# Rotary embedding of q: cosine and sine products summed by GpSimd ahead of a smaller product with the 192 rows

## The reference

```
# D=256, K=128 per head, D_CQ=192, D_C=64, R=64
q_hk   = (hidden_q @ Wq.T)                      # per head 128
q_big  = einsum('bshk,hkq->bshq', q_hk, w_kc_q) # per head 192
q_big  = q_big*cos + rotate_half(q_big)*sin     # 192 rows, halves of 96
kv_r   = rope(kv_c)                             # 64
q_r    = einsum('bshq,hqr->bhsr', q_big, W_qr)  # per head 64
k_r    = einsum('bld,hdr->bhlr', kv_r, W_kr)
attn   = softmax(einsum('bhsr,bhlr->bhsl', q_r, k_r))
ctx    = einsum('bhsl,bld->bhsd', attn, kv_r)   # then w_kc_kv and Wo
```

## Time and profile before

| | |
|---|---|
| median of 3 runs | 559.76 us (558.8 to 560.43) |
| span of the profiled execution | 556.6 us |
| TensorE (PE) busy | 514.5 us, 92% |
| VectorE (DVE) busy | 416.5 us, 75% |
| ScalarE (ACT) busy | 307.4 us, 55% |
| GpSimd (POOL) busy | 153.4 us, 28% |
| chain that ended last | PE 64%, DVE 22% |

### The profile page before, as it was taken

The page is one execution under the profiler, slowest core; times in us unless marked ns, Lnnn a source line. Parts: engine busy times, 40 slices in busy tenths (PEclk is TensorE's granted clock), DMA queues, the critical chain, the costliest instruction groups (busy, mean ns, idle before and its releaser), DMA issues.

```text
span 556.6 us, 9071 instructions
## 1 busy us (share of the span) xinstructions
PE 514.5 (92%) x2842; PEld 391.6 (70%) x2842; DVE 416.5 (75%) x1106; ACT 307.4 (55%) x766; POOL 153.4 (28%) x152
## 2 busy tenths in 40 slices
PE   6888899998988998799999999999999988799995
PEld 3766678776867885467777777777776766588874
DVE  5988799977677668998888888888887875544322
ACT  3743654424544542577777777776777744055541
POOL 0042456755435721000000000010000007335560
PEclk9959999999999999899999999999999997999998
DMA  8668612222412329581708080807004602334426
GB/s 258 199 181 283 206 58 85 86 71 72 140 60 70 102 56 241 112 198 34 168 24 181 13 190 9 194 11 167 0 2 168 298 1 95 96 90 121 134 67 226
DMA packets 40280, 66.34 MB, mean 119 GB/s; under 512 B 4323, under 2 KB 30637, under 8 KB 39984
## 3 DMA queue, kind: packets, MB, share of 16 engines
q1 hardware_dynamic: 37984, 61.62, 39.6%
q0 software_dynamic: 2256, 4.21, 2.4%
HBM read 39.40 MB, written 28.39 MB: 122 GB/s over the span
## 4 chain that ended last, share of the span: by engine, by line
PE 64%; DVE 22%; DMA 4%; ACT 4%; issue 3%; POOL 1%; SPq 1%; POOLq 0%; DVEq 0%
PE bank L1524 10%; PE bank L792 8%; PE bank L1544 5%; PE bank L1595 5%; PE bank L1582 5%; PE bank L1571 4%; PE bank L996 4%; PE bank L827 3%; PE bank L1561 3%; PE bank L1548 2%; PE bank L1562 2%; DVE xn L355 2%; PE bank L1012 2%; DMA moe_x<-xn_slots 2%; DVE hid L748 2%
## 5 line engine op out<-in xcount | busy, mean ns | idle before, releaser
L1744 ACT ACTIVATE silu<-bank,negm 128x256 f32<-128x256 f32 x128 | 59.4, 472 | 10.3 <-DVE negm L2019 10.2
L1396 POOL TENSOR_TENSOR att_w_l<-att_w_raw,att_w_h 128x384 fp32r<-128x384 f32 x16 | 16.7, 1047 | 146.0 <-ACT att_w_h L1773 146.0
L2019 DVE TENSOR_REDUCE negm<-bank 128x2 f32<-128x512 f32 x64 | 43.9, 686 | 13.5 <-PE bank L1562 13.0
L709 POOL TENSOR_TENSOR ffn_w_l<-ffn_raw,ffn_w_h 128x512 fp32r<-128x512 f32 x30 | 39.6, 1322 | 47.5 <-ACT ffn_w_h L721 47.3
L733 ACT ACTIVATE hid_h<-hid 128x512 fp32r<-128x512 f32 x28 | 17.7, 631 | 54.9 <-DVE hid L748 49.2
L1757 ACT ACTIVATE probsT<-bank 128x512 f32<-128x512 f32 x64 | 38.0, 593 | 12.6 <-PE bank L1571 11.2
L1561 PE MATMUL bank<-ks_h,qs 128*128 128x256 f32 x128 | 40.5, 340 | 3.7 <-ACT silu L1744 2.1
L1751 ACT ACTIVATE hid<-silu,rden 128x256 f32<-128x256 f32 x55 | 27.8, 506 | 23.1 <-DVE rden L2024 23.1
L1571 PE MATMUL bank<-ident,hid 128*128 128x128 f32 x256 | 38.9, 275 | 1.2 <-DVE hid L2029 0.8
L792 PE MATMUL bank<-xT_h,ffn_w_h 128*128 128x512 f32 x120 | 39.5, 410 | 0.0
L951 POOL DMA_INDIRECT y_rows<-moe_y,route_rows x31 | 30.2, 973 | 32.8 <-issue 16.8
(11 more groups left out here) (247 smaller groups left out, 1347.6 us busy)
## 6 DMA issues: line engine op xcount, KB each, us to landing
xn_slots<-blank SPq DMA_DIRECT2D x8, 2056.0 KB, 12.8
ffn_raw<-in_w_ffn SPq DMA_DIRECT2D x30, 256.0 KB, 2.6
pair_w<-in_pair_w SPq DMA_DIRECT2D x8, 768.0 KB, 6.0
moe_w<-in_w_moe SPq DMA_DIRECT2D x1, 6144.0 KB, 18.0
folds<-att_w_raw SPq DMA_DIRECT2D x6, 704.0 KB, 7.2
moe_x<-xn_slots SPq DMA_DIRECT2D x31, 128.5 KB, 2.1
ffn_raw<-in_w_ffn SPq DMA_DIRECT2D x30, 128.0 KB, 2.3
att_w_raw<-folds SPq DMA_DIRECT2D x6, 384.0 KB, 12.1
```

Source lines behind the costliest of these rows:

```text
L709: nc.gpsimd.tensor_tensor(wt_l[b][:, 0:GU], raw[b][:, 0:GU], wt_h[b][:, 0:GU], ALU.subtract).then_inc(self.wgl, 1)
L1744: last = nc.scalar.activation(ex[u % 2][:, h, :], bank[4 + u % 2][:, h * S:(h + 1) * S], ACT.Exp, bias=negm[:, u % 2, h:h + 1], accum_out= ...
L2019: nc.vector.tensor_reduce(negm[:, u % 2, :], bank[4 + u % 2][:].rearrange("p (h n) -> p h n", h=2), AX_X, ALU.max, negate=True).then_inc(s ...
```

## The change

The sum of cosine and sine product, which TensorE made by adding up in PSUM, is made by GpSimd. For that the sine product has to lie on the partitions of its partner, so the 192 rows of each head are put in another order (`turned_order`): row r and its partner r +- 96 are 64 partitions apart in each tile. The order is applied to the weights and the tables on the host.

- `cos_sin`: every tile gets one product with cosine over 128 partitions into plane 0, and two products with sine over 64 partitions, each written to the other half's partitions of plane 1.
- `turned` (new, GpSimd): plane 0 += plane 1, 128x512, one per tile, 48 in all; in slot n for the tile of VectorE's slot n-1, ahead of `low_part`. The six of pair 0 stand before and after the splits of the next layer's weights.
- `rope_step`: two steps of two matmuls instead of three, on plane 0; they wait for `turned`.
- Folds: G has 4 blocks of 64 columns instead of 6; `fold` makes four products instead of six. `fold_out` copies the q product in two pieces per k (256 and 128 columns, rearranged) instead of one of 384. The rope weights' input shrinks from 896 to 640 columns over 64 partitions, the stored fold from 1408 to 1280 columns.

Normalising, the softmax, the values and the output are as they were.

```diff
-PR = 2 * 2 * CQ + 2 * C
+PR = 4 * P + 2 * C
-FOFF = GOFF + 2 * JT * C
+FOFF = GOFF + 4 * C
...
+                def turned(i, n):
+
+                    pool.wait_ge(s_cs, i * (4 * JT) + 2 * (n + 1))
+                    nc.gpsimd.tensor_tensor(qr[n][:, 0, :], qr[n][:, 0, :], qr[n][:, 1, :],
+                                            ALU.add).then_inc(s_turned, 1)
+
                 def slot(n, lap):
+                    tile = lap.cos_tile(n - 1)
+                    if tile is not None:
+                        turned(lap.i, tile)
                     m = lap.weights(n)
...
+                turned(0, 0)
+                turned(0, 1)
                 for st in (ffn1_first, ffn1_second):
                     ffn1.low_gateup(pool, st)
+                for n in range(2, 2 * JT):
+                    turned(0, n)
                 run_laps(slot, pool, {})
...
-                    for g in range(2 * JT):
-                        h = (0, 0, 0, 1, 1, 1)[g]
+                    for g in range(4):
+                        h = g % 2
                         nc.tensor.matmul(bank[4][:, g * C:(g + 1) * C], pr[b][:, g * P:(g + 1) * P],
...
-                    whole = [c * JT + m for m in range(JT) if J_OF[m] != 1]
-                    mixed = [c * JT + m for m in range(JT) if J_OF[m] == 1][0]
-                    for w in range(2):
-                        pe.wait_ge(s_cs, i * 12 + (2 * whole[1] + w + 1))
-                        for h, n in enumerate(whole):
-                            nc.tensor.matmul(bank[2][h * C:(h + 1) * C, :], g_of(w_raw[p], 4 * h + w),
-                                             qr[n][:, w, :], start=(w == 0), stop=False, skip_group_check=True)
-                    pe.wait_ge(s_cs, i * 12 + (2 * mixed + 2))
+                    for h in range(2):
+                        pe.wait_ge(s_turned, i * (2 * JT) + (c * JT + h + 1))
+                        nc.tensor.matmul(bank[2][h * C:(h + 1) * C, :], g_of(w_raw[p], h),
+                                         qr[c * JT + h][:, 0, :], start=True, stop=False, skip_group_check=True)
+                    pe.wait_ge(s_turned, i * (2 * JT) + (c * JT + JT))
                     for h in range(2):
                         last = nc.tensor.matmul(bank[2][h * C:(h + 1) * C, :], g_of(w_raw[p], 2 + h),
-                                                qr[mixed][:, h, :], start=False, stop=True, skip_group_check=True)
+                                                qr[c * JT + 2][:, 0, :], start=False, stop=True, skip_group_check=True)
...
-                        nc.scalar.activation(f[:, k * 2 * CQ:(k + 1) * 2 * CQ], bank[2 + k][:, 0:2 * CQ],
+                        heads = bank[2 + k][:, 0:2 * CQ].rearrange("p (h q) -> p h q", h=2)
+                        own, mixed = f[:, k * 2 * CQ:k * 2 * CQ + 2 * P], f[:, k * 2 * CQ + 2 * P:(k + 1) * 2 * CQ]
+                        nc.scalar.activation(own.rearrange("p (h q) -> p h q", h=2), heads[:, :, 0:P], ACT.Copy)
+                        nc.scalar.activation(mixed.rearrange("p (a h c) -> p a h c", a=2, h=2),
+                                             heads[:, :, P:CQ].rearrange("p h (a c) -> p a h c", a=2),
                                              ACT.Copy).then_inc(s_fcp, 1)
...
-                    if j == 1:
-                        for h in range(2):
-                            hs = slice(h * C, (h + 1) * C)
-                            for w, tab in ((0, cosq), (1, sinq)):
-                                last = nc.vector.tensor_tensor(
-                                    to[h][w * C:(w + 1) * C, :, :], q2[hs, :, :],
-                                    tab[hs, j:j + 1, :].broadcast_to([C, 2, S]), ALU.mult)
-                            last.then_inc(s_cs, 1)
-                    else:
-                        for w, tab in ((0, cosq), (1, sinq)):
-                            nc.vector.tensor_tensor(to[w], q2, tab[:, j:j + 1, :].broadcast_to([P, 2, S]),
-                                                    ALU.mult).then_inc(s_cs, 1)
+                    j = n % JT
+                    by_cos, by_sin = [qr[n][:, w, :].rearrange("p (b s) -> p b s", b=2) for w in range(2)]
+                    nc.vector.tensor_tensor(by_cos, q2, cosq[:, j:j + 1, :].broadcast_to([P, 2, S]),
+                                            ALU.mult).then_inc(s_cs, 1)
+                    for h in range(2):
+                        hs, other = slice(h * C, (h + 1) * C), slice((1 - h) * C, (2 - h) * C)
+                        last = nc.vector.tensor_tensor(by_sin[other, :, :], q2[hs, :, :],
+                                                       sinq[hs, j:j + 1, :].broadcast_to([C, 2, S]), ALU.mult)
+                    last.then_inc(s_cs, 1)
```

More of the change, by code:

```diff
@@ L256, in build @@
             "stack_l_ready")
+        s_turned = sem("q_turned_tile_ready")
         s_sc, s_nm, s_ex, s_rd, s_tr, s_ev = sems(
@@ L1187, in batch_of @@
             return 2 * half_of(i, b // 2) + b % 2
-        J_OF = (0, 2, 1)
         Q_AT, FIRST_Q_AT = {0: 1, 1: 2, 3: 3, 4: 4, 5: 5}, {1: 2, 3: 3, 4: 4, 5: 5}
@@ L1426, in fold @@
                         pe.wait_ge(s_fcp, 4 * i)
-                    for g in range(2 * JT):
-                        h = (0, 0, 0, 1, 1, 1)[g]
+                    for g in range(4):
+                        h = g % 2
                         nc.tensor.matmul(bank[4][:, g * C:(g + 1) * C], pr[b][:, g * P:(g + 1) * P],
-                                         pr[b][:, 4 * CQ + h * C:4 * CQ + (h + 1) * C], start=True, stop=True)
+                                         pr[b][:, 4 * P + h * C:4 * P + (h + 1) * C], start=True, stop=True)
                     for h in range(2):
@@ L1509, in q_step @@
                 def q_step(i, b, n):
-                    c, j = n // JT, J_OF[n % JT]
+                    c, j = n // JT, n % JT
                     bk = bank_of(i, n)
@@ L1993, in cos_sin @@
                     q2 = bank[bank_of(i, n)][:].rearrange("p (b s) -> p b s", b=2)
-                    j = J_OF[n % JT]
-                    to = [qr[n][:, w, :].rearrange("p (b s) -> p b s", b=2) for w in range(2)]
-                    if j == 1:
-                        for h in range(2):
-                            hs = slice(h * C, (h + 1) * C)
-                            for w, tab in ((0, cosq), (1, sinq)):
-                                last = nc.vector.tensor_tensor(
-                                    to[h][w * C:(w + 1) * C, :, :], q2[hs, :, :],
-                                    tab[hs, j:j + 1, :].broadcast_to([C, 2, S]), ALU.mult)
-                            last.then_inc(s_cs, 1)
-                    else:
-                        for w, tab in ((0, cosq), (1, sinq)):
-                            nc.vector.tensor_tensor(to[w], q2, tab[:, j:j + 1, :].broadcast_to([P, 2, S]),
-                                                    ALU.mult).then_inc(s_cs, 1)
+                    j = n % JT
[7 more added lines that the diff above has]
+                    last.then_inc(s_cs, 1)
                 def q_low(i, b, c):
@@ L2133, in rope_tables, with turned_order @@
     return np.repeat(np.sin(f), 2, axis=-1).astype(np.float32), np.repeat(np.cos(f), 2, axis=-1).astype(np.float32)
+def turned_order():
+    half, whole = CQ // 2, P // 2
+    a = np.arange(half)
+    return np.concatenate([a[:whole], half + a[:whole], a[whole:], half + a[whole:]])
 def constants():
@@ L2141, in constants @@
     sq_m = (sq[:, turned] * sign[None, :]).T
-    pack = lambda t: np.concatenate([t, t]).reshape(JT, P, S).transpose(1, 0, 2)
+    own = turned_order()
+    tail = own[P:].reshape(2, 32)
+    pack = lambda t: np.stack([t[own[0:P]], t[own[0:P]], t[np.repeat(tail, 2, axis=0).reshape(-1)]], axis=1)
     sk, ck = rope_tables(S, C)
@@ L2202, in layouts @@
     wo = v["L1_xattn_Wo"].T.reshape(H, KH, D)
-    turned = (np.arange(CQ) + CQ // 2) % CQ
+    own = turned_order()
     pw, pr = [], []
@@ L2206, in layouts @@
         h0, h1 = 2 * i, 2 * i + 1
-        pw.append(np.concatenate([wq[h0], wq[h1], v["L1_xattn_w_kc_q"][h0], v["L1_xattn_w_kc_q"][h1],
+        pw.append(np.concatenate([wq[h0], wq[h1], v["L1_xattn_w_kc_q"][h0][:, own], v["L1_xattn_w_kc_q"][h1][:, own],
                                   v["L1_xattn_w_kc_kv"][h0], v["L1_xattn_w_kc_kv"][h1], wo[h0], wo[h1]], axis=1))
@@ L2210, in layouts @@
         kr = [v["L1_xattn_W_kr"][h].T for h in (h0, h1)]
[L2211 to L2214, removed]
+        mixed = np.zeros((2, R, 2, 2, 32), np.float32)
+        for h in range(2):
+            mixed[h, :, :, h, :] = qr[h][:, own[P:]].reshape(R, 2, 32)
+        pr.append(np.concatenate([m[:, own[0:P]] for m in qr] + list(mixed.reshape(2, R, P)) + kr, axis=1))
     g["pair_w"] = np.stack(pw)
```

## The result

| | before | after |
|---|---|---|
| median of four runs each | 559.67 us (558.8 to 560.43) | 584.26 us (579.36 to 586.55) |
| ratio, with its 95% interval | | 1.0457 (1.0407 to 1.0506) |
| span of the profiled execution | 556.6 us | 584.3 us |
| its granted clock, mean over the span | 0.972 | 0.956 |

The kernel became 4.6% slower; 577.6 us (+3.2%) was forecast, with a range of 564 to 586. The profiled execution after took 586.27 us, so 2.0 lie around its span, and it is itself 2.0 above the median. The four runs after spread more than those before, along with the clock: the shortest has a span of 577.4 at a mean of 0.976, the profiled one 584.3 at 0.956.

The account below looks back on a forecast made before the run. TensorE was taken to bound the kernel. Span: 556.6 + 0.4 + 4.4 + 14.7 + 0.7 - 0.9 - 1.5 = 574.4 us; with 3.2 around it 577.6 us (+3.2%), range 564 to 586.

Parts of the forecast that it names:

- The threshold: Attention half-lap (three q tiles, four slots): over 1.06 us added to VectorE's work makes the kernel slower.
- VectorE's ring: VectorE's half-lap without waits for TensorE's scores: 13.13 us before the change, against TensorE's 14.19.
- Rival (c): In the half-laps TensorE stays the bound, VectorE at 13.29 us against 13.26: 547 us in all; 5%.
- A rope step of 0.93: Each rope call on TensorE loses one step of 0.93 us, sixteen times; TensorE's half-lap becomes 13.26 us.
- Products of 2.12 per tile: VectorE's three cosine and sine products wait at each start-partition change: 0.69 + 0.70 + 0.73 = 2.12 us per tile.
- rival (a): Half-row products wait but adds stop nothing: half-laps of 14.54 us, about 563 us in all; 7%.
- The two stops: GpSimd's adds hold up VectorE's normalising in slots 2/6 and 3/7: 0.24 + 0.75 us per half-lap.
- rival (b): Only slot 2's stop happens, normalising getting in 0.16 us ahead of the add in slot 3: 568 us; 13%.
- Eleven half-laps: Attention loop after the first lap: each half-lap 1.34 us longer, 15.53 against 14.19; +14.7 us together.
- The entry: Before VectorE's first maximum of the laps: two tiles' delays less what the rope step and mixed tile return, +0.4 us.
- Rival (d): TensorE's waits in the half-laps lower its clock, +11 us for each wholly at 1.2 GHz: 589 to 600 us; 9%.
- First lap: From VectorE's first maximum through the eight slots of the first lap: 28.8 us instead of 24.43, +4.4.

Follow-up runs that it names:

- e5: Kernel after, with ScalarE normalising both heads instead of one in the shared laps: 556.99 us, 0.9983 of the kernel before.
- e8: Kernel before, with ScalarE normalising both heads instead of one in the shared laps: 559.01 us, ratio 1.0004.
- e4: Kernel after, with one sine product over 128 partitions, not exchanging halves (output not the reference's): 547.67 us, 0.9814 of the kernel before.
- e9: Kernel after, with both heads normalised on ScalarE in shared laps, nine zero matmuls at the entry, maximum ahead of q's low part: 551.96 us, 0.9891.
- e1: Kernel after, with each GpSimd add cut from 512 columns to 2 (output not the reference's): 565.67 us, 1.0133 of the kernel before.
- e3: Kernel after, with each add in the laps also waiting for the normalising it would collide with: 567.53 us, 1.0165 of the kernel before.
- e6: Kernel after, with nine matmuls of zeros in TensorE's wait ahead of the laps: 582.06 us, 1.0432 of the kernel before.
- e2: Kernel before, plus 48 GpSimd adds of 128x512 that nothing reads, released by the products: 573.62 us, ratio 1.029.
- e11: Kernel before, with only the maximum put ahead of q's low part in slots 3 and 7: 561.33 us, ratio 1.0044.

## Why the prediction held, and where its sizes were off

**The bound changes hands.** The threshold was 1.06 us per half-lap on VectorE's ring. The edit adds more, VectorE takes over the chain, and TensorE idles for 17 us of 150. Shown by the windows, and from both sides by e5 and e8. Rival (c), TensorE stays the bound, fell in the kernel as changed. Its price, 547 of 559.76 us (0.977), is nearly reached by e4 (0.981) and not by e9 (0.989); the half-lap of 13.29 it needs is seen only in e4's last three (13.36).

**A rope step of 0.93.** It was read as half of the 1.87 in the earlier trace rows, and the first piece of such a run of products comes out long in the chain: the third step of the same call takes 0.86 in the chain (260.79 to 261.65). By starts, a call of three steps takes 2.62 us (258.86 to 261.48) and one of two steps 1.77 (266.46 to 268.23 in the kernel after). So TensorE's half-lap would be 13.34, not 13.26. As TensorE is not the bound in the loop, little of the result hangs on it.

**Products of 2.12 per tile.** They take 2.14, in steps of 0.72 and then 1.42 for two, and 0.20 follows ahead of the maximum. The bound of 0.60 for each did not come true. With the stops gone (e1, e3) the half-lap is 14.6, where 14.54 was worked out for rival (a): this part alone is past the threshold, by 0.4 where 0.3 was said. The Trainium skill (VectorE: DVE Perf Modes, "Two Vector instructions with no wait between them") has instructions held at a change of start quarter; the trace agrees, with 0.70 to 0.72 against e4's 0.60. That the instructions have only 64 partitions is not the reason: in the earlier trace rows a product over 64 follows the normalising after 0.26 (259.61 to 259.87), as one over 128 does (257.49 to 257.75).

**The two stops.** In the half-lap shown they are in the slots where they were placed, and in no other. In slot 3 normalising loses to an add that starts 0.16 ahead of it (271.36 and 271.52), as forecast and against rival (b). The term was 0.24 + 0.75 = 0.99 and measured 0.32 + 0.94 = 1.26. Most of the difference is the add itself: 1.29 us, not the 1.18 of the earlier trace rows, which was taken for its size; 1.30 was the bound. Twice 0.11 is 0.22 of the 0.27. The value from another form of the instruction was the wrong end to take.

**Eleven half-laps: +14.7 forecast, +18.4 measured.** That is 0.34 each: 0.27 the stops, 0.07 the rest. Slots 3.79, 3.86, 3.52, 4.73 against 3.72, 3.84, 3.42, 4.55. This is the largest single part of the miss of 6.7 us.

**The entry: +0.4 forecast, +3.0 measured.** The step that failed outright is the sum for the entry (two tiles of 0.92 each, less the rope step and the mixed tile, plus the wait of the low part): it added up the delays and left out TensorE's clock. As a sum of delays it is right. In e6, where the clock stays at 1.00, it is 20.58 us from the first q product to the first maximum (206.24 to 226.82), in the kernel before 20.18 (207.71 to 227.89): +0.40. In the kernel after the clock is at the lower level behind the wait, and that makes the 2.6 us by which the entry missed. Rival (d) looked for this inside the half-laps, where the clock held at 1.00, and not ahead of them.

**First lap: +4.4 forecast, +5.4 measured.** The clock of 0.66 from 232 to 242 lies within it, but it is not the reason: e6 has 0.99 from 228 to 240 and takes as long from its first maximum to q's third low part (226.82 to 253.41, 26.6 us; 230.33 to 256.93 in the kernel after). The stops are longer here as in the loop. The largest single difference is slot 5, 3.98 us for 3.60: its normalising takes 1.12 (at 248.71), under an add that lasts until 249.68.

**The end.** The four slots to the last rope call cost 2.0 and not 0.7, as both stops fall among them. The last rope call was to be 0.9 shorter and is not. The first two of its four products in the kernel after and in e6:

```profile
450.62 1.92 PE L1554 MATMUL bank<-qr,att_w_raw 128*64 128x512 f32 x4
...
446.31 1.08 PE L1554 MATMUL bank<-qr,att_w_raw 128*64 128x512 f32 x4
```

The granted clock is 0.83 from 445 to 455 us in the first and 1.00 in the second, and the next step starts 1.75 and 0.91 us behind. At the full clock the call is 0.85 shorter than the one before; the low clock took that back.

**The opening: -1.5 forecast, -0.6 measured.** The fold's rope weights went from 1.48 (twelve) to 1.03 (eight), as said. The rest was given back, in the main where six matmuls of the opening (L448) took 2.73 us instead of 1.55, at a clock of 0.53 from 57 to 60. They take 2.73 in all nine kernels with the smaller folds, and with the old folds 1.55 or 1.56 in three (before, e2, e8) and 2.73 in one (e11). So the change seems to have a part in it; through what was not tried.

**The sum.** In spans 574.4 was forecast and 584.3 measured: 2.6 of it at the entry, 1.0 in the first lap, 3.7 in the half-laps, 2.2 at the end, 0.9 in the opening, and 0.5 back behind the last call. Around the span lie 2.0 us and not 3.2, and the profiled execution is 2.0 above the median: 9.9 - 1.2 - 2.0 = 6.7. The mechanism was right, and in its range the forecast was also lucky: nearly all the misses point the same way, 584.26 lies 1.7 below the end of the range, and two of the four runs (586.27 and 586.55) lie beyond it.

## What to carry to other kernels

When work is moved off the bounding engine, compare the ring of the next engine, without the waits that would vanish, with the bound: the difference (here 1.06 us per half-lap) is all that can be won, and all that the helpers may add. Work handed to GpSimd was free here where VectorE's instructions took an operand from PSUM meanwhile, and not under one from SBUF to SBUF; one more semaphore wait that moves it from the normalising to the products was worth about 16 of the 25 us lost. A wait of TensorE that grows is to be priced with the clock, too: 2.6 us here for 0.95 more of waiting, and a fill of idle products took them back.

## What the runs showed of the hardware

- A GpSimd addition stops VectorE's normalising (SBUF to SBUF): 1.29 us instead of 0.34 at 271.52, done 0.16 behind the add's end. Over products that read PSUM the same add costs nothing: 0.71 + 1.42 us in e3.
- When two GpSimd instructions stand back to back, a normalising is let in between in some cases and not in others. It took 0.95 us in e2 where it came 0.80 ahead of the first one's end (232.47; likewise at 243.99), and 1.44 where it came 0.05 ahead (261.77, and three more times in e2, four in e4). The Trainium skill (SBUF — State Buffer, "SBUF: two separate sides") has the lock held for one whole instruction; the rows agree. In the eight cases of 0.05 to 0.06 GpSimd went first each time; why is not shown, and GpSimd's times in a trace are rough.
- GpSimd's fp32 addition of 128x512 takes 1.18 us in one place and form (`x<-x,xn` at 33.05) and 1.29 in another (`qr<-qr`, two planes of one tile; 1.28 for `att_gap<-ks_h`). What makes the difference was not tried.
- At the entry, a wait of TensorE of 2.68 us was followed by the lower clock in four kernels of four, one of 1.73 in two of five, and with nine products of zeros in the wait the clock stayed at 1.00 in four of four.
